# The transform back in runs of 128 columns and two 64-row tiles, the biases added to x on GpSimd, and the bias products between the runs

## The chip, the cores and the metric

The kernel runs on one core of one Trainium2 chip. The time is the device time of one execution in microseconds: 444.74 us in the median of 3 runs (444.65 to 445.85). The instructions and the queues of the five engines are written out by hand: PE is TensorE, ACT is ScalarE, DVE is VectorE, POOL is GpSimd, and SP only issues DMAs.

## The reference, cut to what matters

```
xf  = rfftn(gn(x).reshape(B, H, W, 4, 96), axes=(H, W), norm='ortho')      # 8 images, 32 x 32, 384 channels
r1  = relu(xr @ w1[0] - xi @ w1[1] + b1[0]);  i1 = relu(xr @ w1[1] + xi @ w1[0] + b1[1])
r2  = r1 @ w2[0] - i1 @ w2[1] + b2[0]
i2  = r2 @ w2[1] + i1 @ w2[0] + b2[1]                                       # r2 enters again
out = x + irfftn(r2 + 1j * i2) + gn(x) @ bias_w.T + bias_b                  # gn: 32 groups over H, W and 12 channels
```

Every float32 product is done as three float16 products of a high and a low part: high by high, high by low, low by high.

## The kernel before, in words

One image is one pass of `image(b, p)`, which each engine has for itself; semaphores alone tie the engines together, and each engine takes its instructions in the order written. On PE an image runs through these stages. `c1` multiplies y, the width transform of the normalised x, with w1. `p3_half` and `p3_last` transform along the height. `p1` already transforms the next image along the width. `p4` (L649) is the transform back: it takes r, the spectrum after the relu, as stationary and the table `heightT` as moving operand, so that the channels come to lie on the partitions, and makes rho. `c2_bias` (L688) multiplies y with the bias map, 18 products in pairs of 64-column tiles. `c2_rho` (L708) multiplies rho with w2 for each of 8 tiles gi. `mean` and `variance` of the next image stand between them, and `p6` ends the image.

p4 has ten runs j. The first eight take 96 columns of r each, which is one block of channels in its real or imaginary part, with 4 units by 3 products of 128 columns; the last two take unit 8, six products of 132 columns each. After each run ACT makes the high part of rho out of PSUM (L881, L887) and then DVE the low part (L1078, L1084). In the middle and at the end of the eight a copy of 12 columns moves on each of them (L884, L1081). A run waits for the evacuation of the run four before it (L667). One bias tile stands ahead of run 4 (L654), two behind run 9 (L751), and then PE waits for the whole of rho (L753).

DVE does `r_low(7)` and `r_low(8)` right ahead of its part of p4 (L1068, L1069). The bias vectors ride along in c2_rho: rows 96 to 98 of rho hold marks, loaded once (L502), and rows 96 to 98 of w2s hold b2 and bias_b (K = 99 in place of 96, L717).

Ahead of the first image DVE and POOL build w2f, the four forms of w2, with products on PE (L774 to L779, L805 to L807, L1161 to L1170). POOL finds the largest value over all partitions twice, with PARTITION_ALL_REDUCE (L800 and L814); the second one needs `largest_weight` and `largest_bias` of DVE (L1172, L1177), and DVE's `second_scales`, ACT's `weight_high` of the bias map and the rest of the first image need it. The output is made by `add_x` (L1032) out of the p6 product and x_sb, the x of this image. SP loads x of image b + 2 once image b is stored. Behind the last w1, w2, bias, table, b1 and x loads of the start SP issues eight small mark loads.

## Time and profile before

| what | value |
|---|---|
| median of 3 runs | 444.74 us |
| profiled execution, span from first to last instruction | 443.0 us |
| PE busy | 411.8 us (93%), 7832 products |
| PE weight loads busy | 375.5 us (85%) |
| DVE, ACT, POOL busy | 318.4 us (72%), 239.8 us (54%), 7.2 us (2%) |
| DMA | 32.50 MB, 20.1% of the 16 engines' time |
| bias products (1152), rho with w2 (3072) | 108.8, 84.5 us busy |
| transform back, p4 (864) | 52.3 us busy |

The median lies 1.7 us above the span: starting and ending a program is in it. A row of a group gives its line, its engine, what it writes and reads, the shapes, the count, the busy time, the mean of one and the idle time ahead of it with what ended that. A row of the timeline gives start and length in us. Products overlap, so the mean length of one (206 ns, say) is not its price; the price is the distance from start to start.

### The profile page before, as it was taken

Reading aid. Unit: us, or ns where it says so; the run is one execution under the profiler, and the core shown is the slowest. Engines: PE = TensorE matmul, PEld = TensorE weight load, DVE = VectorE, ACT = ScalarE, POOL = GpSimd, SP = SyncE. Lnnn points to the kernel's source line nnn. Section 1 sums busy time; section 2 is a strip of 40 time slices with the busy share of each in tenths; the row PEclk is TensorE's granted clock in tenths of the full one; section 3 lists DMA queues with packets and bytes.
Section 4 is the critical chain, followed back from the end, with each engine's and each line's share of the span. In section 5 each row is a group of like instructions: output and inputs, shape, how many; then the busy total and the mean of one; then the engine's idle time right before and its main releaser. Section 6 shows DMA issues by size and latency. Waiting matters only on the chain.

```text
span 443.0 us, 17840 instructions
## 1 busy us (share of the span) xinstructions
PE 411.8 (93%) x7832; PEld 375.5 (85%) x7832; DVE 318.4 (72%) x772; ACT 239.8 (54%) x568; POOL 7.2 (2%) x13
## 2 busy tenths in 40 slices
PE   4468699989999999999999999999999999998996
PEld 4457699889998899888998899888998899987894
DVE  3679895759776876769767786768857687668734
ACT  2654785257742685438752586438752577425620
POOL 0131000000000000000000000000000000000000
PEclk9759899999999999999999999999999999999999
DMA  7570000170004300170003500161002600030004
GB/s 216 164 216 2 2 1 4 63 261 3 3 23 157 148 1 5 38 285 3 3 12 123 194 1 4 38 243 45 2 5 88 236 1 4 27 155 3 4 4 144
DMA packets 11645, 32.50 MB, mean 73 GB/s; under 512 B 4196, under 2 KB 5904, under 8 KB 11568
## 3 DMA queue, kind: packets, MB, share of 16 engines
q1 hardware_dynamic: 11568, 31.36, 20.1%
q8 instruction: 62, 1.02, 1.0%
q14 instruction: 15, 0.12, 0.1%
HBM read 15.63 MB, written 12.58 MB: 64 GB/s over the span
## 4 chain that ended last, share of the span: by engine, by line
PE 81%; issue 7%; DVE 6%; SPq 2%; POOL 2%; ACT 1%; DVEq 0%; POOLq 0%
PE bank L535 81%; SPq L490 1%; DVE r L1022 1%; DVE z L947 1%; DVE rsum L1015 1%; SPq L495 1%; POOL g L806 1%; ACT biasw L857 1%; DVE o_sb L1037 0%; DVE rho L947 0%; POOL g L807 0%; ACT z L863 0%; ACT yraw L823 0%; DVE extreme L1175 0%; DVE extreme L1180 0%
## 5 line engine op out<-in xcount | busy, mean ns | idle before, releaser
L535 PE MATMUL bank<-biasw,y 128*64 128x384 f16 x1152 | 108.8, 335 | 0.0
L535 PEld LDWEIGHTS bank<-biasw,y 128*64 128x64 f16 x1152 | 93.5, 196 | 1.7 <-DVE rsum L1015 0.3
L535 PEld LDWEIGHTS bank<-w2s,rho 96*64 96x64 f16 (+1 forms) x3072 | 81.4, 109 | 4.4 <-issue 2.5
L535 PE MATMUL bank<-w2s,rho 96*64 96x96 f16 (+1 forms) x3072 | 84.5, 207 | 0.0
L863 ACT ACTIVATE z<-bank 128x384 f16<-128x384 f32 x72 | 35.2, 488 | 60.5 <-PE bank L535 59.9
L535 PE MATMUL bank<-w1R,y 128*32 128x96 f16 (+3 forms) x768 | 60.1, 228 | 7.6 <-ACT y L843 3.2
L848 ACT ACTIVATE g<-bank 128x384 f16<-128x384 f32 x64 | 31.0, 484 | 64.2 <-PE bank L535 64.2
L535 PE MATMUL bank<-tab,x_sb 128*128 128x128 f32 x384 | 52.5, 291 | 11.2 <-DMA x_sb<-in_x 6.6
L535 PEld LDWEIGHTS bank<-tab,x_sb 128*128 128x128 f32 x384 | 48.3, 201 | 14.6 <-issue 7.4
L947 DVE SCALAR_TENSOR_TENSOR rho<-bank,rho 96x64 f16<-96x64 f32 (+1 forms) x128 | 50.6, 431 | 10.9 <-PE bank L535 9.2
L947 DVE SCALAR_TENSOR_TENSOR z<-bank,z 128x384 f16<-128x384 f32 x72 | 39.9, 557 | 25.6 <-ACT z L863 25.2
L1029 DVE SCALAR_TENSOR_TENSOR g<-g,bank 128x384 f16<-128x384 f16 x64 | 34.8, 552 | 28.0 <-ACT g L848 27.6
L535 PE MATMUL bank<-w1I,y 128*128 128x192 f16 (+1 forms) x384 | 53.6, 249 | 0.0
L535 PEld LDWEIGHTS bank<-tab,r 128*96 128x96 f16 (+1 forms) x864 | 50.8, 124 | 2.5 <-issue 1.8
L535 PE MATMUL bank<-tab,r 128*96 128x128 f16 (+2 forms) x864 | 52.3, 221 | 0.4 <-DVE rsum L1015 0.4
L535 PEld LDWEIGHTS bank<-w1R,y 128*32 128x32 f16 (+3 forms) x768 | 38.2, 98 | 12.8 <-issue 7.8
L853 ACT ACTIVATE r<-rsum 128x384 f16<-128x384 f32 (+1 forms) x72 | 37.2, 519 | 9.9 <-DVE rsum L1015 9.1
L881 ACT ACTIVATE rho<-bank 96x480 f16<-96x480 f32 x64 | 35.1, 564 | 13.5 <-PE bank L535 9.5
L1037 DVE SCALAR_TENSOR_TENSOR o_sb<-bank,unscale,x_sb 128x384 f32<-128x384 f32 x64 | 35.0, 610 | 7.9 <-PE bank L535 7.9
L1022 DVE SCALAR_TENSOR_TENSOR r<-rsum,r 128x384 f16<-128x384 f32 (+1 forms) x72 | 37.4, 549 | 3.4 <-ACT r L853 2.7
L1015 DVE SCALAR_TENSOR_TENSOR rsum<-bank,b1s 128x384 f32<-128x384 f32 (+1 forms) x72 | 38.2, 547 | 0.0
L947 DVE SCALAR_TENSOR_TENSOR y<-yraw,rstd,y 128x1024 f16<-128x1024 f32 x24 | 30.9, 1292 | 8.0 <-ACT y L843 7.8
(102 smaller groups left out, 379.0 us busy)
## 6 DMA issues: line engine op xcount, KB each, us to landing
x_sb<-in_x SPq DMA_DIRECT2D x16, 768.0 KB, 7.1
out<-o_sb SPq DMA_DIRECT2D x14, 768.0 KB, 3.8
y<-y SPq DMA_DIRECT2D x24, 128.0 KB, 2.7
out<-o_sb SPq DMA_DIRECT2D x8, 192.0 KB, 1.9
tab<-in_tab SPq DMA_DIRECT2D x1, 642.0 KB, 5.9
o_sb<-in_bias_wt SPq DMA_DIRECT2D x4, 144.0 KB, 2.8
b1s<-in_b1h SPq DMA_DIRECT2D x1, 384.0 KB, 5.3
o_sb<-in_w SPq DMA_DIRECT2D x2, 144.0 KB
```

Source lines behind the costliest of these rows:

```text
L490: sp.dma_start(dst, src).then_inc(w1_in, 16)
L495: sp.dma_start(dst, src).then_inc(w2_in, 16)
L535: return nc.tensor.matmul(o, lhsT, rhs, start=start, stop=stop, **kw)
L848: nc.scalar.activation(g[:, 0, gi, :], g_bank(gi, more)[:, 0:CH], ACT.Copy, scale=G_EVAC).then_inc(gh_ready, 1)
L853: nc.scalar.activation(r[0:rows, 0, u, :], rsum[0:rows, u, :], ACT.Relu).then_inc(rh_ready, 1)
L863: nc.scalar.activation(z[:, 0, u, :], b_bank[u % 3][:, 0:CH], ACT.Copy, scale=Z_EVAC).then_inc(zh_ready, 1)
L881: nc.scalar.activation(rho_columns(0, j), rho_sums(bank), ACT.Copy, scale=H_EVAC).then_inc(rhoh_ready, 1)
L947: return nc.vector.scalar_tensor_tensor(out=out, in0=value, scalar=factor, in1=high, op0=ALU.mult, op1=ALU.subtract)
L1015: nc.vector.scalar_tensor_tensor(out=rsum[0:rows, u, :], in0=spec_bank(u)[0:rows, 0:CH], scalar=H_EVAC, in1=b1s[0:rows, u // 4, :], op0=AL ...
L1022: nc.vector.scalar_tensor_tensor(out=r[0:rows, 1, u, :], in0=rsum[0:rows, u, :], scalar=0.0, in1=r[0:rows, 0, u, :], op0=ALU.max, op1=ALU. ...
L1029: nc.vector.scalar_tensor_tensor(out=g[:, 1, gi, :], in0=g[:, 0, gi, :], scalar=-1 / G_EVAC, in1=g_bank(gi, more)[:, 0:CH], op0=ALU.mult, ...
L1037: nc.vector.scalar_tensor_tensor(out=o_sb[:, t, :].rearrange("k (p q) -> k p q", q=4), in0=o_bank[t % 4][:, 0:CH].rearrange("k (q p) -> k ...
```

## The change

In p4 the eight runs of 96 columns of r become six of 128 (j = 0 to 5, tile j % 3 of half j // 3). Each product is split into rows 0 to 63 and rows 64 to 127, with half of the table's columns each (64), into two banks that lie side by side; so a run has 24 products of 64 columns in place of 12 of 128. Unit 8 takes two runs (j = 6 and 7) with 24 products of 96 columns each, whose output tiles are 64 or 32 partitions wide. rho has three tiles of 128 partitions for each half in place of four blocks of 96. ACT reads one run with one instruction of 512 elements, DVE with two (256 and 224). The bias tiles stand ahead of runs 2, 4 and 6, and none behind the last run. c2_rho keeps its 48 products for each gi, now with 128 rows, some of them zero.

The marks and their rows go. What b2 and bias_b add to the output is a row for image row 0 and one for the others; PE and DVE work it out at the start (`shift_loads`, five float32 products, `shift_rows`, `shift_all`), and POOL adds it to x_sb in place for each image, once p1 has read it: one instruction of 384 and one of 2688 elements. add_x waits for that. The forms of w2 are all built by DVE, in 12 instructions (`second_forms`), and POOL's three instructions for them go. Loads at the start: w2 comes in twelve as before, but with 0.88 MB in place of 0.59; the float32 constants grow by 0.13 MB, and three loads (bias_all is 0.2 MB, b2col is 384 single words) replace the eight small ones of the marks.

```diff
+LOAD_PIECES = ((0, 0, 96, 0, 0, 0), (0, 96, 128, 0, 1, 0), (1, 0, 64, 0, 1, 32), (1, 64, 128, 1, 0, 0), (2, 0, 32, 1, 0, 64), (2, 32, 128, 1, 1, 0))
+WIDE_PIECES = ((0, 0, 64, 0, 0, 0), (1, 0, 64, 0, 1, 32), (1, 64, 128, 1, 0, 0), (2, 64, 128, 1, 1, 32))
+SMALL_PIECES = ((0, 64, 96, 0, 0, 64), (0, 96, 128, 0, 1, 0), (2, 0, 32, 1, 0, 64), (2, 32, 64, 1, 1, 0))
...
         def rho_bank(j, more):
+            if j < 6:
+                at = (2, 0 if more else 4)[j % 2]
+                return psum[:, at:at + 2, :]
+            return (b_bank[2] if more else c_bank[1], b_bank[0])[j - 6]
...
+            yield w2imag[:, :, :], w2[1].rearrange("b k n -> k b n")
+        def shift_loads():
+            yield b2rows[:, :], b2.rearrange("a b n -> a (b n)")
+            yield b2col[:, :], b2[0].rearrange("b n -> n b")
+            yield bias_all[:, :], bias_b.rearrange("(o n) -> o n", o=1).to_broadcast([128, CH])
...
+                        pe.wait_ge(w2_forms, 12)
+                        pe.wait_ge(added_ready, 6)
...
+                for j in range(8):
+                    if j in (2, 4, 6):
+                        gi = j // 2 - 1
+                        if more:
+                            c2_bias(b, p, gi, more, first)
+                        elif gi:
+                            c2_bias(b, p, 3 - gi, more, first)
+                    if j == 0:
+                        pe.wait_ge(spec_sum, 9 * b + 6)
+                    elif j == 1 and more:
+                        pe.wait_ge(y_raw, Y_ITEMS * (b + 1) + 5)
+                    elif j == 1:
                         pe.wait_ge(zh_ready, 9 * b + 9)
                         pe.wait_ge(zl_ready, 9 * b + 9)
+                        pe.wait_ge(spec_sum, 9 * b + 7)
+                    elif j < 6:
+                        pe.wait_ge(rhoh_ready, 8 * b + j - 1)
+                        pe.wait_ge(rhol_ready, 8 * b + j - 1)
+                    elif j == 6 and more:
+                        pe.wait_ge(y_raw, Y_ITEMS * (b + 2))
+                    elif j == 6:
+                        pe.wait_ge(spec_sum, 9 * b + 8)
+                    else:
+                        pe.wait_ge(rhoh_ready, 8 * b + 5)
+                        pe.wait_ge(rhol_ready, 8 * b + 5)
+                    if j in (0, 3, 6):
+                        pe.wait_ge(rh_ready, 9 * b + (4, 8, 9)[j // 3])
+                        pe.wait_ge(rl_ready, 9 * b + (4, 8, 9)[j // 3])
                     bank = rho_bank(j, more)
+                    if j < 6:
+                        ti = j % 3
                         for t in range(4):
+                            u = 4 * (j // 3) + t
+                            for of, w in ((0, 0), (0, 1), (1, 0)):
+                                for h in range(2):
+                                    rows = slice(64 * h, 64 * h + 64)
+                                    table = heightT[rows, w, int(u in SHORT_UNITS), :].rearrange("k (t c) -> k t c", t=TILES)[:, :, 8 * h:8 * h + 8]
+                                    o = bank[:, h, 0:256].rearrange("k (c u m) -> k c u m", u=4, m=4)[:, :, t, :]
+                                    last = mm(o, r[rows, of, u, 128 * ti:128 * ti + 128], table, of == 0 and w == 0, of == 1, skip_group_check=True)
                     else:
+                        half = j - 6
+                        for pieces in (WIDE_PIECES, SMALL_PIECES):
+                            for of, w in ((0, 0), (0, 1), (1, 0)):
+                                for tile, first_row, last_row, k, ri, ch in pieces:
+                                    at = BC * (2 * half + k) + ch
+                                    last = mm(bank[first_row:last_row, 0:384].rearrange("k (a t c) -> k a t c", a=3, c=32)[:, :, tile, :],
+                                              r[:, of, 8, at:at + last_row - first_row], xi[:, w, 96 * ri:96 * ri + 96], of == 0 and w == 0 and tile in (0, 1) and first_row == 64 * tile, of == 1, skip_group_check=True)
                     last.then_inc(rho_prod, 1)
...
+                                mm(columns[64:128], rhoX[:, of, half, tile, :], w2s[:, w, half, 0, slot, :], False, False, skip_group_check=True)
                             for part in range(2):
                                 at = 16 * (1 - part)
+                                last = mm(columns[64 * part:64 * part + 64], rho[:, of, half, tile, gi, at:at + 64],
+                                          w2s[:, w, half, part, slot, :], False, half == 1 and slot == 3 and of == 1, skip_group_check=True)
                 last.then_inc(g_prod, 1)
...
-                for gi in range(1, 3 if more else 2):
-                    c2_bias(b, p, gi, more, first)
-                pe.wait_ge(rhoh_ready, 10 * b + 10)
-                pe.wait_ge(rhol_ready, 10 * b + 10)
+                pe.wait_ge(rhoh_ready, 8 * b + 8)
+                pe.wait_ge(rhol_ready, 8 * b + 8)
...
+            for pieces in (WIDE_PIECES, SMALL_PIECES):
+                for tile, first_row, last_row, k, ri, ch in pieces:
+                    for half in range(2):
+                        blk = 2 * half + k
+                        last = mm(w2_product(tile)[first_row:last_row, half, :], w2T[:, blk, ri, ch:ch + last_row - first_row],
+                                  w2imag[:, blk, :], True, True, skip_group_check=True)
+            last.then_inc(w2_prod, 1)
+            pe.wait_ge(shift_in, 16 * N_SHIFT)
+            pe.wait_ge(added_ready, 1)
+            mm(c_bank[2][:, 0:CH], T("impulse", 2), b2rows[:, :], True, False, skip_group_check=True)
+            for blk in range(BLOCKS):
+                last = mm(c_bank[2][:, BC * blk:BC * blk + BC], b2row0[:, blk, :], w2imag[:, blk, :], False, blk == BLOCKS - 1, skip_group_check=True)
...
-            pool.wait_ge(w2_in, 16 * N_W2)
-            pool.wait_ge(consts_in, 16)
-            do(nc.gpsimd.tensor_copy(w2_form(0, BC, 0), by_group(w2raw[0:BC, :, 0, :])))
-            do(nc.gpsimd.tensor_scalar(w2_form(0, BC, 1), by_group(w2raw[0:BC, :, 1, :]), -1.0, None, ALU.mult))
-            do(nc.gpsimd.tensor_scalar(w2_form(BC, 3, 0), by_group(w2raw[BC:BC + 3, :, 0, :]), rowscale[BC:BC + 3, :], None, ALU.mult))
             pool.wait_ge(second_largest, 2)
-            do(nc.gpsimd.tensor_copy(extreme[BC:BC + 3, 4:5], extreme[BC:BC + 3, 2:3]))
-            do(nc.gpsimd.memset(extreme[BC:BC + 3, 2:3], 0.0))
             pool.wait_ge(s1_ready, 1)
-            do(nc.gpsimd.tensor_tensor(extreme[:, 2:5], extreme[:, 2:5], coef[:, 2:5], ALU.mult))
-            do(nc.gpsimd.tensor_scalar(extreme[:, 3:5], extreme[:, 3:5], s1[:, :], None, ALU.mult))
-            all_peak(extreme[:, 2:5], peaks2[:, :])
+            do(nc.gpsimd.tensor_tensor(extreme[:, 2:4], extreme[:, 2:4], coef[:, 2:4], ALU.mult))
+            do(nc.gpsimd.tensor_scalar(extreme[:, 3:4], extreme[:, 3:4], s1[:, :], None, ALU.mult))
+            all_peak(extreme[:, 2:4], peaks2[:, :])
+            pool.wait_ge(added_ready, 6)
+            for b in range(BATCHES):
+                pool.wait_ge(y_prod, Y_ITEMS * (b + 1))
+                tiles = x_sb[b % 2]
+                nc.gpsimd.tensor_tensor(tiles[:, 0, :], tiles[:, 0, :], added[:, 0, :], ALU.add).then_inc(x_shifted, 1)
+                nc.gpsimd.tensor_tensor(tiles[:, 1:TILES, :], tiles[:, 1:TILES, :], added[:, 1:2, :].to_broadcast([128, TILES - 1, CH]), ALU.add).then_inc(x_shifted, 1)
...
                     dve.wait_ge(stored[t // 4], 16 * b + 16)
...
+                    if j < 6:
+                        low(rho_columns(1, j)[:, 0], rho_sums(bank)[:, 0], H_EVAC, rho_columns(0, j)[:, 0])
+                        low(rho_columns(1, j)[:, 1, :, 0:28], rho_sums(bank)[:, 1, :, 0:28], H_EVAC, rho_columns(0, j)[:, 1, :, 0:28]).then_inc(rhol_ready, 1)
+                        if j % 3 == 2:
...
-                dve.wait_ge(pool_prep, 3)
+                dve.wait_ge(w2_prod, 1)
+                for part in range(2):
+                    for slot, tile, first_row, last_row in ((0, 0, 0, 128), (1, 1, 0, 64), (2, 1, 64, 128), (3, 2, 0, 128)):
+                        rows = slice(first_row, last_row)
+                        to, signs = w2_form(first_row, last_row, part, slot), sign[rows, tile:tile + 1]
+                        if part == 0:
+                            nc.vector.tensor_scalar(to, by_group(w2raw[rows, :, tile, :]), signs, None, ALU.mult).then_inc(w2_forms, 1)
+                            continue
+                        for half in range(2):
+                            nc.vector.scalar_tensor_tensor(out=to[:, half], in0=by_group(w2_product(tile)[rows])[:, half], scalar=signs,
+                                                           in1=by_group(w2real[rows, :, tile, :])[:, half], op0=ALU.mult, op1=ALU.add).then_inc(w2_forms, 1)
+            def shift_rows():
+                dve.wait_ge(shift_in, 16 * N_SHIFT)
+                row0 = T("row0", BC).rearrange("k (o m) -> k o m", o=1).to_broadcast([BC, BLOCKS, 128])
+                nc.vector.tensor_tensor(b2row0[:, :, :], row0, b2col[:, :].rearrange("k (b o) -> k b o", o=1).to_broadcast([BC, BLOCKS, 128]),
+                                        ALU.mult).then_inc(added_ready, 1)
+            def shift_all():
+                dve.wait_ge(shift_prod, 1)
+                for a in range(2):
+                    for of in range(2):
+                        parts = []
+                        for v in (added[:, a, :], bias_all[:, :], c_bank[2][:, 0:CH]):
+                            if len(parts) == 0:
+                                v = v.rearrange("k (c i q) -> k c i q", c=3, q=4)
+                                parts.append(v[:, :, :, 0:3] if of == 0 else v[:, :, :, 3])
+                            elif of == 0:
+                                parts.append(v[:, 0:3 * BC].rearrange("k (c i q) -> k c i q", c=3, q=3))
+                            else:
+                                parts.append(v[:, 3 * BC:CH].rearrange("k (i c) -> k c i", c=3))
+                        if a == 0:
+                            made = nc.vector.tensor_tensor(parts[0], parts[1], parts[2], ALU.add)
+                        else:
+                            made = nc.vector.tensor_copy(parts[0], parts[1])
+                        made.then_inc(added_ready, 1)
+                nc.vector.memset(newton[:, 0:1], 0.0).then_inc(added_ready, 1)
             def largest_weight():
+                dve.wait_ge(w2_forms, 12)
...
             image(0, 0, first=True)
             for b in range(1, BATCHES - 1):
```

## Rows read from the trace of the kernel before

**Rows 1.** The page: the span and the chain that ended last
```profile
span 443.0 us, 17840 instructions
...
PE 81%; issue 7%; DVE 6%; SPq 2%; POOL 2%; ACT 1%; DVEq 0%; POOLq 0%
```

**Rows 2.** Timeline of one image's transform back (start us, us, engine line, what)
```profile
207.23 2.85 PE L535 MATMUL bank<-tab,r 128*96 128x128 f16 x48
208.34 2.35 ACT L881 ACTIVATE rho<-bank 96x480 f16<-96x480 f32 x4
209.01 2.43 DVE L947 SCALAR_TENSOR_TENSOR rho<-bank,rho 96x480 f16<-96x480 f32 x4
210.01 1.74 PE L535 MATMUL bank<-biasw,y 128*64 128x384 f16 x18
211.48 0.26 DVE L1081 COPY rho<-rho 96x384 f16<-96x384 f16 x1
...
215.21 3.20 PE L535 MATMUL bank<-biasw,y 128*64 128x384 f16 x36
...
218.24 0.21 PE L535 MATMUL bank<-w2s,rho 99*64 99x96 f16 x1
```

**Rows 3.** Weight loads in groups, shapes kept apart (busy us, mean ns, then idle before)
```profile
L535 PEld LDWEIGHTS bank<-tab,r 128*96 128x96 f16 x672 | 43.5, 124 | 2.5 <-issue 1.8 <-DVE rsum L1015 0.7
...
L535 PEld LDWEIGHTS bank<-w1I,y 128*128 128x128 f16 x288 | 25.9, 100 | 0.2
```

**Rows 4.** Timeline of PE: rho with w2, products in two column tiles
```profile
221.97 1.23 PE L535 MATMUL bank<-w2s,rho 99*64 99x96 f16 x48
```

**Rows 5.** DVE in groups, shapes kept apart: the low part of rho
```profile
L947 DVE SCALAR_TENSOR_TENSOR rho<-bank,rho 96x480 f16<-96x480 f32 x64 | 39.9, 650 | 9.7 <-PE bank L535 9.2
...
L947 DVE SCALAR_TENSOR_TENSOR rho<-bank,rho 96x64 f16<-96x64 f32 x64 | 10.7, 212 | 1.2 <-ACT rhoX L887 1.2
```

**Rows 6.** Timeline of POOL at the start
```profile
16.90 0.86 POOL L805 COPY g<-o_sb 96x384 f32<-96x384 f32 x1 [4.26 <-issue]
26.21 2.55 POOL L806 TENSOR_SCALAR g<-o_sb 96x384 f32<-96x384 f32 x1 [8.45 <-issue]
28.86 1.58 POOL L807 TENSOR_SCALAR g<-o_sb,tab 3x384 f32<-3x384 f32 x1
...
38.88 0.68 POOL L812 TENSOR_TENSOR extreme<-extreme,tab 128x3 f32<-128x3 f32 x1
39.66 0.31 POOL L813 TENSOR_SCALAR extreme<-extreme,s 128x2 f32<-128x2 f32 x1
```

**Rows 7.** Chain that ended last: between POOL's L813 and its second all-reduce (peaks, L797)
```profile
40.21 6.00 issue
```

**Rows 8.** Timeline of DVE beside POOL at the start
```profile
27.27 1.52 DVE L947 SCALAR_TENSOR_TENSOR y<-yraw,rstd,y 128x1024 f16<-128x1024 f32 x1
...
38.70 0.81 DVE L1148 TENSOR_SCALAR b1s<-b1s,s 128x1152 f32<-128x1152 f32 x1
```

**Rows 9.** Group of those y instructions at the start, min/median/max ns
```profile
L947 DVE SCALAR_TENSOR_TENSOR y<-yraw,rstd,y x3: 1277/1285/1523, 24.9 to 27.3; 128x1024 f16<-128x1024 f32 x3
```

**Rows 10.** Timeline at the start: products for w2, the forms, the first z
```profile
21.34 2.91 PE L535 MATMUL bank<-o_sb,g 96*99 96x96 f32 x16
...
32.83 0.58 DVE L1170 TENSOR_SCALAR g<-o_sb,tab 3x384 f32<-3x384 f32 x1
33.45 1.02 DVE L947 SCALAR_TENSOR_TENSOR z<-bank,z 128x384 f16<-128x384 f32 x2
```

**Rows 11.** Windows: length, busy us (x) by engine, granted clock, DMA share, GB/s
```profile
25.00:30.00 5.00, 2.55 (x17) 2.38 (x18) 3.79 (x3) 2.27 (x3) 3.69 (x2) 0.50 0.90 306
30.00:35.00 5.00, 3.21 (x33) 2.92 (x31) 4.32 (x7) 1.03 (x3) 0.44 (x1) 0.89 0.12 36
```

**Rows 12.** Timeline of the next image's variance: its input on DVE, its use on PE
```profile
223.38 0.16 DVE L984 TENSOR_REDUCE qv<-qv 128x1 f32<-128x3 f32 x1
...
225.69 0.61 PE L535 MATMUL bank<-qv,tab 128*128 128x3 f32 x4
```

More of the change, by code:

```diff
@@ L188, in constants @@
     put("const", np.broadcast_to(const, (128, 64)))
-    tab[96:99, TAB["rowscale"][0]] = [ROOT, ROOT, 8.0]
-    put("coef", np.broadcast_to([1, 2.0 ** -8, 1, 2.0 ** -7, 2.0 ** -11], (128, 5)))
-    mark = np.zeros((3, TILES, 2, 2, 16))
-    mark[0, 0, 0, 0, :] = 1
-    mark[0, 0, 0, 1, 15] = 1
-    mark_a = mark.copy()
-    mark_a[1, 0, 0, 0, 15] = 1
-    mark_a[2, :, :, 0, 15] = 1
-    mark_a[2, 0, 0, 0, 15] = 0
-    mark_b = mark.copy()
-    mark_b[0, 0, 0, :, 15] = 0
-    extra = np.zeros((3, 64))
-    extra[1, 12] = 1
-    units_a, units_b = (m.reshape(3, TILES, 4, 4, 4).transpose(0, 1, 3, 4, 2).reshape(3, TILES, 4, 16) for m in (mark_a, mark_b))
-    marks = np.concatenate([np.concatenate([units_b[:, :, 3:4], units_a], axis=2).reshape(3, 640), extra], axis=1)
+    sign = np.ones((128, 3))
+    for tile, first, last, _, ri, _ in LOAD_PIECES:
+        if ri:
+            sign[first:last, tile] = -1
+    put("sign", sign)
+    put("coef", np.broadcast_to([1, 2.0 ** -8, 1, 2.0 ** -7], (128, 4)))
+    whole = np.ones((SIDE, SIDE // 2 + 1))
+    real, imag = (np.fft.irfftn(c * whole, s=(SIDE, SIDE), norm="ortho")[0] for c in (1, 1j))
+    impulse = np.zeros((2, 128))
+    impulse[0, 0:SIDE] = real
+    impulse[1, 0:SIDE] = imag
+    put("impulse", impulse)
+    put("row0", np.broadcast_to(impulse[1], (BC, 128)))
+    marks = np.zeros((1, 2))
     tab = tab.astype(np.float32)
@@ L234, in spectral_block_kernel @@
         r = sb("r", [128, 2, 9, CH], f16)
[L235 to L236 removed]
+        rho = sb("rho", [128, 2, 2, 3, TILES, 80], f16)
+        rhoX = sb("rhoX", [128, 2, 2, 3, 64], f16)
         g = sb("g", [128, 2, TILES, CH], f16)
@@ L409, in bias_loads @@
             yield biasraw[3:128:4, :, :], bias_wt[288:384, :].rearrange("(i b) n -> i b n", b=3)
[L411 to L416 removed]
+        N_W1, N_B1, N_W2, N_BIAS, N_SHIFT = (len(list(loads())) for loads in (w1_loads, b1_loads, w2_loads, bias_loads, shift_loads))
         N_ZERO = 6
@@ L501, in _ @@
             load(1, 1)
-            for dst, src in mark_loads():
-                sp.dma_start(dst, src).then_inc(marks_in, 16)
+            with nc.allow_non_contiguous_dma(reason="one column of 96 per block"):
+                for dst, src in shift_loads():
+                    sp.dma_start(dst, src).then_inc(shift_in, 16)
             def store(b, tiles=TILES // 2):
@@ L649, in p4 @@
             def p4(b, p, more, first):
-                for j in range(10):
-                    if j == 4:
-                        c2_bias(b, p, 0 if more else 2, more, first)
-                    if j == 3 and more:
-                        pe.wait_ge(y_raw, Y_ITEMS * (b + 2))
-                    elif j in (3, 4) and not more:
-                        pe.wait_ge(spec_sum, 9 * b + 4 + j)
-                    elif j < 2:
-                        pe.wait_ge(spec_sum, 9 * b + 5 + j)
-                    elif j == 2 and more:
-                        pe.wait_ge(spec_sum, 9 * b + 4)
-                    elif j == 2:
+                for j in range(8):
[10 more added lines that the diff above has]
+                    elif j == 1:
@@ L1201, in _ @@
             second_forms()
+            shift_rows()
+            shift_all()
             image(0, 0, first=True)
```

173 lines of the change are left out of this document (66 added, 107 removed).

## The prediction

> **What bounds the kernel now.** I read the page first: PE holds 81% of the chain that ended last, and what is left, DVE, POOL and time in which nothing is seen to be waited for, lies at the start [rows 1]. So a change counts where it shortens PE's queue or holds it up. Then the timeline of one image's transform back [rows 2]: its first product starts at 207.23 and the first of c2_rho at 218.24, 11.0 us later, and PE has no idle time in between. The double bias tile at 215.21 (3.20 us) covers the evacuation of the last runs. Then the start, where PE does not set the pace: DVE first reaches z at 33.45 [rows 10], and the second all-reduce on POOL waits 6.00 us in which nothing runs [rows 7].
>
> **Part 1, the products of p4.** Now 48 products take 2.85 us with the length of one, 0.22, at the end [rows 2], so 56 ns each: 128 columns at 2.4 GHz are 53. In c2_rho 48 products of 96 columns, two column tiles at a time, take 1.23 us with 0.21 at the end [rows 4]: 22 ns each, 43 a pair, where 96 columns are 40. So a pair costs its columns and some 3 ns, and the weight loads of both tiles lie beside that. A pair of the new products streams 64 columns in two row tiles: 29 ns, and a run of 12 pairs 0.35 us. The trace of before has no tiles of 64 rows by 128 columns; the other bound is that the 128 weights load at one column a cycle, 53 ns: 56 a pair, 0.67 a run. I take 29, since a load of 128 float16 columns lasts 100 ns and one of 96 columns 124 [rows 3]: a full width already loads in a faster way. Unit 8 has 24 small products a run: 12 at 22 ns, 12 four at a time at 11, and two changes of tile shape at some 0.15 each (a lone bias tile lasts 1.74, half of the double one 1.60 [rows 2]), so 0.68. The bias tiles now all stand alone: 3 x 1.75. PE's own work is 6 x 0.35 + 2 x 0.68 + 5.25 = 8.7 us in place of 11.0.
>
> **Part 2, what gives it back in each image.** No bias tile is left behind the last run, so its evacuation is in the open: 0.2 us until the product is in PSUM, three ACT instructions (0.45; four of 480 elements take 2.35 [rows 2]), three DVE instructions of 96, 96 and 6 elements (0.4; DVE takes 212 ns for 64 elements and 650 for 480, so 1.05 ns an element [rows 5]) and the semaphores, 1.15 us together. DVE can't start on rho before r_low(8) is done, at 209.01 [rows 2]; at 0.70 us a run (256 and 224 elements) it lets run 2 start at 209.8 and run 3 at 210.5, 0.45 us later than PE alone would. POOL slows DVE a little beside this (below), 0.2 to 0.3. Sum 10.6: **0.4 us less an image**, with bounds of 1.1 less (no waits on DVE, a short tail) and 1.0 more (56 ns a pair). c2_rho keeps its 48 products of 96 columns; 128 rows in place of 96 or 99 change nothing. The variance of the next image isn't late next: its input is there at 223.38 and PE takes it at 225.69 [rows 12].
>
> **Part 3, POOL's additions.** They are released when p1 is through; its last product ends at about 207.4, just as p4's first is under way [rows 2], and add_x needs them only at the image's end, so POOL's own time is hidden. What they do to DVE isn't. Price: a copy of 384 elements takes 0.86 us [rows 6], so 2688 take 6.0; by the row of 1.58 us for 384 it would be 11.1. I take 6.0, since these operands lie in order as that copy's nearly do. The two instructions then run until 214.4. (The Trainium skill, GPSIMD Engine Reference, section 3.1, gives 4497 ns for a tensor_tensor of 2048 float32 elements; by that it would be an estimated 5.9 us, and the sum stays.) On DVE L1148 does 1152 float32 elements in 0.81 us, faster than 1.05 ns an element [rows 8], and POOL's L812, three elements, starts under it at 38.88 and lasts 0.68, until DVE is done, while L813 right behind takes 0.31 [rows 6]. So a fast DVE instruction out of SBUF into SBUF and a POOL instruction exclude each other. In p4 DVE has one such: the copy L1081, 384 float16 elements in 0.26 [rows 2], now behind run 2's low part, at some 211.8. It would wait until 214.4; then come 0.2 for it and 0.7 for run 3's low part, until 215.3. Run 5 waits for that and would have started at 213.05. So **2.25 us are added, net 1.85 in each of the seven images** that hold additions for the next one. By POOL's two prices this is 0.4 to 7 us; in the last image 0.4 us are saved.
>
> **Part 4, the start.** (a) The forms of w2: DVE no longer waits for POOL's (28.86 + 1.58 [rows 6]) and starts at 28.8, as soon as the last y is done. Twelve instructions, by 0.58 for 384 elements [rows 10] some 0.36 for each of the four and 0.27 for each of the eight short ones, last until 32.3. Then shift_rows waits for its three loads, queued behind all others. The loads of before end at some 30.6 us (306 GB/s until 30, 36 GB/s after that [rows 11]); 0.3 to 0.6 MB more put that at 32 to 33.3. shift_rows (512 elements, 0.6), five float32 products on PE at half clock [rows 11] (16 of 96 columns took 2.91 [rows 10]; these are eight times 96 columns, 1.5), and shift_all (768 elements out of PSUM and SBUF, 1.5) end at 37.4. Queued behind these stand DVE's z and PE's c1, which now comes behind the five products. z started at 33.45: **4.0 us later**; bounds 2.5 (loads landed, short products) and 6. (b) POOL took 8.45 us ahead of L806 without a recorded reason, and 6.00 us ahead of the second all-reduce [rows 6, 7], each time where the kind of instruction changes between all-reduce and tensor operations; the copy L805 had none beyond its loads. I read that as code being fetched. Before, the first one lay under loads. Now the first tensor operation of POOL is the multiplication behind `second_largest`, so the fetch comes there, in front of everything that waits for the scales, and the second fetch stays. **6.0 us**, less 0.4 for the two small instructions dropped: 5.6. If the fetch is done ahead of that wait it costs nothing; I hold that for one in four.
>
> **The sum.** The profiled execution has 443.0, and 1.7 around it: 444.7, as the median. 444.7 + 4.0 + 5.6 + 7 x 1.85 - 0.4 = 466.9. The case's own range is 460 to 473.
>
> **Rivals.**
> R1, POOL disturbs nothing: no exclusion in this direction. For it: POOL's L806 ran beside a DVE instruction that then took 1523 in place of 1277 ns, 0.25 more and no wait of its length [rows 6, 8, 9]. Against it: L812. Each image then gains 0.2: 444.7 + 9.6 - 1.4 - 0.4 = 452.5; with the fetch hidden 446.9.
> R2, POOL holds back every DVE instruction with two operands in SBUF: r_low(8), due at some 208.5 as rho follows it at 209.01 [rows 2], would wait until 214.4 and all of rho's low parts with it. That is 5.9 us on the path, 5.5 net: 444.7 + 9.6 + 38.5 - 0.4 = 492. Against it speaks the 0.25 us [rows 9], for it the 2.55 us of L806 where 1.58 was enough for L807 [rows 6]. The Trainium skill (SBUF — State Buffer, section "SBUF: two separate sides") has this as its rule: an exclusive hold for the whole instruction, also against a DVE instruction with two SBUF inputs. The 0.25 us do not bear that out in full.
> R3, the row tiles load weights at one column a cycle, and POOL disturbs nothing: 1.0 more an image, 444.7 + 9.6 + 8.0 = 462.
> R4, the other side: nothing is held, POOL's fetch lies ahead of its wait, and the open tail and DVE's late start are covered, so an image keeps 1.1 us. With the cheap start it is 444.7 + 2.5 - 8.8 = 438. It turns at a start of more than 8 times the gain of an image.
>
> **How the numbers follow.** The forecast 0.38; the same with the fetch hidden (461) 0.10; R1 0.24 (a quarter of it at 447); R2 0.13; R3 0.05; R4 0.10. The range 447 to 490 leaves out R4, half of R2 and a little of R1: about 0.19. A measurement of this kernel can tell some 0.3%, 1.3 us, from no change: faster 0.11, same 0.05, slower 0.84.
>
> **What would show it.** Part 1: runs of 24 products in 0.35 us (plus 0.2 for the last to end), or 0.67. Part 2: some 1.2 us of PE idle ahead of each c2_rho, ended by DVE's rhoX. Part 3: POOL's long instruction at 6 us, DVE's copy behind run 2 starting late or lasting until POOL ends, and PE idle ahead of run 5; r_low as long as before speaks against R2. Part 4: DVE's first z at 37.4 and the second all-reduce's result at 55.8 in place of 46.2, with some 6 us of nothing ahead of POOL's multiplication. The prediction is wrong above all if DVE's copy goes through beside POOL, or if the fetch lies ahead of the wait.

## The result, and the profile after

The changed kernel takes 483.52 us in the median of 4 runs (482.19 to 487.52) beside 444.69 for the kernel before (441.99 to 445.85): a ratio of 1.0895, interval 1.0833 to 1.0957. It is slower by 39 us. The forecast was 467.0, with a range of 447 to 490. The profiled execution has a span of 484.8 us, 41.8 more than before [rows 1]. It was the longest of the four (487.52 us, 4.0 above their median), so the parts below add up to 41.8 us and not to 39.

The page of the changed kernel: span, engines (busy us, share of the span, instructions), the clock in 40 slices, the chain, and the two groups that the rest turns on.

```profile
span 484.8 us, 19207 instructions
PE 410.4 (85%) x8530; PEld 359.6 (74%) x8530; DVE 339.1 (70%) x768; ACT 228.6 (47%) x504; POOL 64.1 (13%) x24
...
PEclk9759968999899998999899998999899998999799
...
PE 67%; DVE 14%; ACT 9%; issue 8%; DMA 1%; DVEq 0%; SPq 0%; ACTq 0%
...
L552 PE MATMUL bank<-tab,r 64*128 64x64 f16 (+2 forms) x1536 | 38.2, 207 | 31.7 <-DVE rho L982 30.5
...
L849 POOL TENSOR_TENSOR x_sb<-x_sb,added 128x2688 f32<-128x2688 f32 x8 | 54.1, 6763 | 0.0
```

p4's products are busy for 38.2 us in place of 52.3, so the part that the change aims at got shorter. But PE now idles 30.5 us ahead of them for DVE's rho, its share of the chain fell from 81% [rows 1] to 67%, and the clock has a dent in each image. The same line of the page of before has one at the start only:

```profile
PEclk9759899999999999999999999999999999999999
```

Where the 41.8 us lie, by the first product of c1 in each image (before 87.8, 139.5, ... 393.16; after 102.64, 158.45, ... 430.87):

| stretch | before | after | more |
|---|---|---|---|
| start to p4 of the first image | 53.47 | 57.71 | 4.24 |
| p4 of the first image, to c2_rho | 11.76 | 22.50 | 10.74 |
| rest of the first image | 22.57 | 22.43 | -0.14 |
| images 1 to 6 | 305.36 | 328.23 | 22.87 |
| last image to the end | 49.84 | 53.93 | 4.09 |

One of the images 1 to 6 in the timeline (start us, us, engine line, what), to be read against [rows 2]:

```profile
175.14 2.40 DVE L1057 SCALAR_TENSOR_TENSOR r<-rsum,r 128x384 f16<-128x384 f32 x3
...
175.50 0.87 PE L552 MATMUL bank<-tab,r 64*128 64x64 f16 x48
...
175.65 1.00 POOL L848 TENSOR_TENSOR x_sb<-x_sb,added 128x384 f32<-128x384 f32 x1 [46.65 <-PE bank L552]
...
176.61 6.68 POOL L849 TENSOR_TENSOR x_sb<-x_sb,added 128x2688 f32<-128x2688 f32 x1
177.46 1.34 DVE L982 SCALAR_TENSOR_TENSOR rho<-bank,rho 128x256 f16<-128x256 f32 x4
178.32 1.11 PE L552 MATMUL bank<-tab,r 64*128 64x64 f16 x48 [0.27 <-DVE rho L982]
...
180.34 3.04 DVE L1118 COPY rho<-rho 128x288 f16<-128x288 f16 x1
...
184.16 0.53 PE L552 MATMUL bank<-tab,r 64*128 64x64 f16 x24 [2.60 <-DVE rho L982]
184.62 3.04 PE L552 MATMUL bank<-biasw,y 128*64 128x384 f16 x18
...
187.45 1.63 PE L552 MATMUL bank<-tab,r 128*64 128x96 f16 x48
...
190.34 0.20 PE L552 MATMUL bank<-w2s,rhoX 128*64 128x96 f16 x1 [1.25 <-DVE rhoX L982]
```

It reads like this. POOL's long addition ends at 183.29. DVE's copy of 288 elements, 0.24 us when alone (the second one of this image, at 186.18), begins at 180.34 and ends at 183.38. The low parts of rho, which read PSUM, run beside POOL at their usual length (four in 1.34 us, at 177.46). Run 5 needs what stands behind the copy, so PE idles 2.60 us. And then comes what the forecast did not have: the bias tile right behind takes 3.04 us in place of 1.74, because PE's clock has fallen. The window of that stretch (length, busy us and count of PE, PEld, DVE, ACT, POOL, granted clock, DMA share, GB/s):

```profile
185.00:190.00 5.00, 4.08 (x66) 2.81 (x62) 1.75 (x8) 2.09 (x9) 0.00 (x0) 0.67 0.01 3
```

The first image, where POOL adds the shift to images 0 and 1 one after the other:

```profile
58.54 1.00 POOL L848 TENSOR_TENSOR x_sb<-x_sb,added 128x384 f32<-128x384 f32 x1 [6.87 <-issue]
...
59.06 8.29 DVE L1057 SCALAR_TENSOR_TENSOR r<-rsum,r 128x384 f16<-128x384 f32 x3
...
59.51 6.15 POOL L849 TENSOR_TENSOR x_sb<-x_sb,added 128x2688 f32<-128x2688 f32 x1
...
66.89 7.92 POOL L849 TENSOR_TENSOR x_sb<-x_sb,added 128x2688 f32<-128x2688 f32 x1
...
69.00 1.34 DVE L982 SCALAR_TENSOR_TENSOR rho<-bank,rho 128x256 f16<-128x256 f32 x4
69.86 1.46 PE L552 MATMUL bank<-tab,r 64*128 64x64 f16 x48 [9.37 <-DVE rho L982]
```

Here r_low itself, with two operands in SBUF, is held: three of 0.55 take 8.29 us. The second long addition takes 7.92 us in place of 6.7; at its start DVE makes the low part of w2s (1.81 us, two operands in SBUF).

The start:

```profile
31.54 0.68 DVE L1216 TENSOR_TENSOR b2row<-tab,b2col 96x512 f32<-96x512 f32 x1
32.37 1.61 PE L552 MATMUL bank<-b2rows,tab 2*128 2x384 f32 x2 [8.34 <-DVE b2row L1216]
33.91 2.02 PE L552 MATMUL bank<-g,b2row 96*128 96x96 f32 x8
35.97 0.69 DVE L1234 TENSOR_TENSOR added<-bias_all,bank 128x288 f32<-128x288 f32 x2 [3.75 <-PE bank L552]
...
38.49 0.56 DVE L982 SCALAR_TENSOR_TENSOR z<-bank,z 128x384 f16<-128x384 f32 x1 [1.42 <-ACT z L898]
...
44.22 0.19 POOL L840 TENSOR_TENSOR extreme<-extreme,tab 128x2 f32<-128x2 f32 x1 [31.21 <-DVE extreme L1248]
...
51.30 0.37 POOL L832 PARTITION_ALL_REDUCE peaks<-extreme  x1 [5.86 <-PE bank L552]
```

The forms of w2 are done at 31.7. z comes at 38.49 in place of 33.45. POOL's multiplication follows DVE's last maximum (ending at 44.07) by 0.15 us, so no fetch lies there; the one ahead of the all-reduce is as long as before, 5.86 us.

### The profile page after: what moved, and what is told of

Its sections match the earlier page's. It is cut to its first block, busy times and chain, and to the rows that moved or that the text cites. A ratio compares the mean times of both kernels' runs of the same rounds, so it can differ in the third digit from the quotient of the medians.

```text
span 484.8 us, 19207 instructions
## 1 busy us (share of the span) xinstructions
PE 410.4 (85%) x8530; PEld 359.6 (74%) x8530; DVE 339.1 (70%) x768; ACT 228.6 (47%) x504; POOL 64.1 (13%) x24
## 4 chain that ended last, share of the span: by engine, by line
PE 67%; DVE 14%; ACT 9%; issue 8%; DMA 1%; DVEq 0%; SPq 0%; ACTq 0%
PE bank L552 67%; DVE r L1057 4%; DVE rho L982 3%; ACT r L888 3%; ACT yraw L858 2%; DVE rsum L1050 2%; DVE z L982 1%; ACT rho L916 1%; DMA x_sb<-in_x 1%; ACT z L898 1%; ACT rho L922 1%; DVE y L982 1%; ACT junk L866 1%; ACT biasw L892 0%; DVE g L1209 0%
## 5 line engine op out<-in xcount | busy, mean ns | idle before, releaser
L552 PE MATMUL bank<-biasw,y 128*64 128x384 f16 x1152 | 119.6, 357 | 0.2 <-DVE biasw L982 0.2
L552 PE MATMUL bank<-w2s,rho 128*64 128x96 f16 x3072 | 83.1, 208 | 0.4 <-issue 0.4
L552 PEld LDWEIGHTS bank<-w2s,rho 128*64 128x64 f16 x3072 | 79.1, 109 | 4.7 <-issue 3.0
L552 PE MATMUL bank<-tab,r 64*128 64x64 f16 (+2 forms) x1536 | 38.2, 207 | 31.7 <-DVE rho L982 30.5
L552 PEld LDWEIGHTS bank<-tab,r 64*128 64x128 f16 (+2 forms) x1536 | 31.9, 104 | 42.4 <-issue 32.2
L982 DVE SCALAR_TENSOR_TENSOR rho<-bank,rho 128x256 f16<-128x256 f32 (+2 forms) x128 | 40.0, 360 | 33.1 <-ACT rhoX L922 17.5
L552 PE MATMUL bank<-w1R,y 128*128 128x192 f16 (+3 forms) x768 | 59.7, 228 | 3.4 <-issue 2.9
L849 POOL TENSOR_TENSOR x_sb<-x_sb,added 128x2688 f32<-128x2688 f32 x8 | 54.1, 6763 | 0.0
L916 ACT ACTIVATE rho<-bank 128x512 f16<-128x512 f32 x48 | 27.4, 592 | 47.0 <-PE bank L552 47.0
L552 PEld LDWEIGHTS bank<-w1R,y 128*128 128x128 f16 (+3 forms) x768 | 38.0, 98 | 6.2 <-issue 4.7
```

Of the source, the lines that this page charges most:

```text
L552: return nc.tensor.matmul(o, lhsT, rhs, start=start, stop=stop, **kw)
L849: nc.gpsimd.tensor_tensor(tiles[:, 1:TILES, :], tiles[:, 1:TILES, :], added[:, 1:2, :].to_broadcast([128, TILES - 1, CH]), ALU.add).then_i ...
L916: nc.scalar.activation(rho_columns(0, j), rho_sums(bank), ACT.Copy, scale=H_EVAC).then_inc(rhoh_ready, 1)
L982: return nc.vector.scalar_tensor_tensor(out=out, in0=value, scalar=factor, in1=high, op0=ALU.mult, op1=ALU.subtract)
```

## The experiments

Each is compared with the kernel before, run on the same chip; ratios carry their 95% interval. p4 means the time from p4's first product to the first of c2_rho in one of the images 1 to 6: 11.01 before, 14.8 after.

**e1_no_add: without POOL's additions.** The loop of POOL and add_x's wait for it are gone; the kernel leaves out what b2 and bias_b add to the output.

```diff
-            for b in range(BATCHES):
-                pool.wait_ge(y_prod, Y_ITEMS * (b + 1))
...
-                dve.wait_ge(x_shifted, 2 * b + (1 if t == 0 else 2))
```

> The changed kernel without POOL's additions and without add_x's wait for them; the output lacks what b2 and bias_b add. Theory A (POOL's instructions shut out DVE, and only that makes the images longer): p4's first product to c2_rho's first falls from 14.8 us to about 10.6, an image from 54.3 to about 50.1 (50.5 in the kernel before), DVE's copy takes 0.24 us, and the kernel 447 to 450 us, the start's 5 us included. Theory B (the new p4 itself, its open tail and the clock that falls behind it, makes the images longer): an image stays above 53 us and the kernel above 470.

450.82 us, ratio 1.0094 (1.0065 to 1.0124). p4 takes 10.23, an image 49.7 us in place of 50.5, and the second image starts at 94.4 (before 87.8, after 102.6). So of 39 us the additions in their place are some 35, by the two ratios. What is left is made of three parts (spans 448.0 and 443.0): +6.6 up to the second image, -5.5 in images 1 to 6, +3.9 in the last. p4 of the first image takes 13.3 here, 11.8 before and 22.5 with the additions: of the 10.7 us more in the table, 9.2 are the additions and 1.5 the new order.

**e2_add_in_c1: the same additions, later.** POOL waits for the next image's c1 in place of p1. A second wait keeps the first image's additions (in eight pieces) behind its rho.

```diff
-                pool.wait_ge(y_prod, Y_ITEMS * (b + 1))
+                if b:
+                    pool.wait_ge(z_prod, 9 * b + 1)
+                else:
+                    pool.wait_ge(rhol_ready, 8)
```

> POOL's additions are released at the first c1 unit of the image whose x they change, not behind its p1; in c1 DVE has no instruction with two SBUF operands and no fast copy. Those of the first image come behind rho in eight pieces. Theory A: as without the additions, within 2 us of that run: 448 to 452 us, with POOL's long instruction at some 6 us and z's low parts as long as before (0.55). A rival C, that POOL slows all of SBUF's users whatever they run: z's low parts, ACT and PE lengthen under it and some 3 us an image stay, 470 us or more.

452.59 us, 1.0122 (1.0058 to 1.0186): 1.3 us more than without additions by the ratios, which is less than their intervals can tell, with the same p4 of 10.23. So the additions cost almost nothing here: it is their place that costs. In c1 DVE makes z and rsum, all of it out of PSUM, and POOL's instruction is shorter there:

```profile
197.62 5.88 POOL L856 TENSOR_TENSOR x_sb<-x_sb,added 128x2688 f32<-128x2688 f32 x1
```

**e3_pieces: the long addition in seven.** Eight instructions of 384 elements, where they stood.

```diff
+                for t in range(TILES):
+                    nc.gpsimd.tensor_tensor(tiles[:, t, :], tiles[:, t, :], added[:, min(t, 1), :], ALU.add).then_inc(x_shifted, 1)
```

> The additions stay behind p1, but in eight instructions of 384 elements of some 1.0 us each, 8 us in all in place of 7.7. If what shuts DVE out lasts as long as one POOL instruction, DVE's copy and r_low wait for one piece at most (1 us or less) and PE's clock does not fall: 0.5 to 1.5 us an image more than without additions, 452 to 462 us. If it is the total work of POOL that counts, 480 us or more.

459.23 us, 1.0266 (1.0210 to 1.0322); p4 11.21. The work on POOL is the same, the hold is not:

```profile
170.77 1.03 DVE L1118 COPY rho<-rho 128x288 f16<-128x288 f16 x1
...
172.58 0.53 PE L552 MATMUL bank<-tab,r 64*128 64x64 f16 x24 [0.59 <-DVE rho L982]
173.03 1.74 PE L552 MATMUL bank<-biasw,y 128*64 128x384 f16 x18
```

The pieces of this image by themselves (ns min/median/max):

```profile
L849 POOL TENSOR_TENSOR x_sb<-x_sb,added x8: 992/1001/1781, 166.1 to 173.6; 128x384 f32<-128x384 f32 x8
```

The copy waits for one piece and gets in between two. PE's wait is 0.59 and the bias tile keeps its 1.74: at this wait the clock stays. POOL goes on adding until 174.6 and DVE and PE go on beside it, so what costs most is the length of one POOL instruction and not how much POOL adds. The pieces still cost 7.6 us by the ratios of e3 and e1, 1.0 in each p4 of the images 1 to 6.

**e4_before_add: the kernel before, with additions of zero.** The two additions of the changed kernel on a tile of zeros, nothing else.

> The kernel before, with POOL adding zeros to x_sb by the same two instructions, released in the same place, and add_x's wait; nothing else changed. Theory A: DVE's copy behind the fourth run (0.26 us) lasts until POOL is done, some 3.5 us later; the double bias tile covers part of it, so 1 to 3 us an image, and several us in the first image, where r_low meets the long instruction: 455 to 470 us. Theory B: within 2 us of the kernel before.

462.1 us, 1.0311 (1.0233 to 1.0388). p4 is 12.2 in place of 11.0, and 23.0 in the first image in place of 11.8. The timeline of an image:

```profile
169.77 6.71 POOL L824 TENSOR_TENSOR x_sb<-x_sb,added 128x2688 f32<-128x2688 f32 x1
...
172.99 3.61 DVE L1092 COPY rho<-rho 96x384 f16<-96x384 f16 x1
...
177.32 0.52 PE L538 MATMUL bank<-tab,r 128*96 128x132 f16 x6 [1.05 <-DVE rho L957]
177.77 3.20 PE L538 MATMUL bank<-biasw,y 128*64 128x384 f16 x36
```

The same hold, 3.61 us, stands in front of PE as 1.05, since the old p4 has more work between the copy and what needs it; the double bias tile keeps its 3.20. So the additions cost the old order 14 us by the ratio (18.9 by the spans, 11.5 of them in the first image) and the new one 35. The difference lies in the images 1 to 6: there they cost the old p4 1.2 us and the new one 4.6. A faster p4 is also a p4 in which PE has less work of its own to put over another engine's delay.

**e5_filler: PE kept busy during its wait.** Sixteen products that nobody reads stand ahead of run 5's wait (in the bank that run 6 writes next, once y has been read out of it).

```diff
+                        if j == 5 and more:
+                            pe.wait_ge(y_raw, Y_ITEMS * (b + 2))
+                            for i in range(16):
+                                mm(b_bank[2][:, 0:CH], inv[:, 0, 1, :], z[:, 0, i % 8, :], True, True)
```

> The changed kernel with 16 products of 384 columns, whose result nobody reads, issued by PE ahead of its wait for run 5, in the bank that run 6 will overwrite: 2.6 us of work in a wait of 2.6 us. The wait stays as it is. If a part of the loss is PE's clock, which falls after that wait, the bias tile behind run 5 goes from 3.04 back to 1.74 us, an image from 54.3 to 52.3 to 52.8, and the kernel from 484 to 468 to 474. If the clock's fall costs nothing or has another cause, the time stays within 3 us of 484.

478.52 us, 1.0754 (1.0695 to 1.0813): above what was expected of the whole, since the first and the last image keep their losses, but the image is as expected, 52.8 in place of 54.3.

```profile
179.88 3.05 DVE L1122 COPY rho<-rho 128x288 f16<-128x288 f16 x1
...
181.03 2.77 PE L552 MATMUL bank<-z,tab 128*128 128x384 f16 x16
...
184.19 1.74 PE L552 MATMUL bank<-biasw,y 128*64 128x384 f16 x18
...
185.76 1.28 PE L552 MATMUL bank<-tab,r 128*64 128x96 f16 x48
```

The copy is held as before (3.05) and run 5 starts as late, but the bias tile takes 1.74 and unit 8's runs 1.28 in place of 3.04 and 1.63. PE did more work and the kernel got faster. So of the 4.6 us that p4 is longer with additions (14.8 against 10.23), 3.0 are the hold (13.26 against 10.23) and 1.5 the clock that falls behind it.

**e6_act_copy: the held copy on ACT.** DVE's two copies (L1118) are made by ACT, the additions stay.

```diff
-                            nc.vector.tensor_copy(rho_third(1, j // 3, 0), rho_third(1, j // 3, 64))
+                            act.wait_ge(rhol_ready, 8 * b + 3)
+                            nc.scalar.activation(rho_third(1, 0, 0), rho_third(1, 0, 64), ACT.Copy)
```

> The changed kernel, but the copy of 12 columns of rho's low part is done by ACT (behind its own part of runs 3 and 6), so that DVE has nothing of the fast kind in p4; POOL's additions stay behind p1. If in the later images the copy alone is shut out, an image falls from 54.3 to 50 to 51, while the first image, where r_low meets the long instruction, stays long: 457 to 462 us. If POOL holds all of DVE's work, an image stays above 53 us.

460.54 us, 1.0346 (1.0281 to 1.0411); p4 10.58.

```profile
176.75 0.44 ACT L922 ACTIVATE rho<-rho 128x288 f16<-128x288 f16 x1
177.45 0.90 PE L552 MATMUL bank<-tab,r 64*128 64x64 f16 x48
178.28 1.74 PE L552 MATMUL bank<-biasw,y 128*64 128x384 f16 x18
```

ACT makes the same copy in SBUF beside POOL in 0.44 us, and run 5 follows run 4 without a wait. This one copy was nearly the whole hold of the images 1 to 6 (10.58 against 10.23 without additions). The first image keeps its 21.4, where r_low is what is held.

**e7_c1_start: e2, with the start rearranged.** The five shift products go behind the third unit of the first c1, `shift_all` behind DVE's fifth z, and p3 waits for it.

> As e2_add_in_c1, and the five float32 products for the added rows stand behind the third c1 unit on PE (which waits for DVE there anyway), shift_all behind scale_b1 on DVE. The start's 5 us consist of PE's wait for those products (3.7 us from shift_rows to shift_all on DVE) and shift_all; this should return 3 to 4.5 us: 447.5 to 449.5 where e2 has 452.6. If the start is set by the second all-reduce's code alone, nothing.

451.33 us, 1.0142 (1.0093 to 1.0192) against e2's 1.0122: the expected return of 3 us and more did not come. c1 starts at 26.49 in place of 36.22, and the shift products take 1.9 us in place of 3.6 (31.86 to 33.80), but then PE stands still until `shift_all` has read their bank:

```profile
39.79 1.07 PE L552 MATMUL bank<-z,tab 32*32 32x384 f16 x45 [3.01 <-issue]
```

The products behind that wait run slowly (45 in 1.07 us, 0.79 in e10). The second image starts 3.2 us earlier in this profile, and that image and the last one give it back (2.3 and 0.9). In the second image PE idles 1.75 us in the middle of c1, where e2 has 0.88 and the profile names no releaser in either:

```profile
103.46 0.20 PE L552 MATMUL bank<-w1R,y 96*32 96x96 f16 x1 [1.75 <-issue]
```

Behind it the clock is lower (0.67 in the window from 105 to 110), which in e2 it is not; 0.9 us of wait and the slow products make up the 2.3.

**e8_c1_start_tail: e7, with the bias tiles placed for cover.** The third bias tile goes behind run 7, where it covers the last evacuation; in the last image the two tiles that are left stand ahead of runs 2 and 4.

```diff
-                    if j in (2, 4, 6):
+                    if j in (2, 4):
...
                 p4(b, p, more, first)
+                if more:
+                    c2_bias(b, p, 2, more, first)
```

> As e7_c1_start, with the third bias tile behind the last run of p4 in place of ahead of run 6, and in the last image bias tiles ahead of runs 2 and 4. The open tail (1.3 us of PE idle ahead of c2_rho) is covered, at the price of 0.2 us of wait ahead of run 7: 0.7 to 1.0 us an image less, and 3 us in the last image, where PE's clock fell: 438 to 442 us, faster than the kernel before. If the tail is set by DVE and not by what PE has to do, an image stays at 49.7 and the kernel at 444 to 446.

444.52 us, 0.9988 (0.9952 to 1.0024): 39 us faster than the changed kernel and level with the one before, but not the 438 to 442 that were expected. p4 is 9.61 in place of 10.23, as expected, and the images behind it take 49.1 to 49.7. What is missing to that lies before: the second image takes 52.3, with 2.04 us of idle time at the same place of c1 as in e7 and a lower clock behind it, and the first one has the start that e10 below mends.

**e11_tail: e2 with that tail alone.**

> This is e2 (additions during c1) with the tail of e8 alone: the third bias tile goes behind p4's run 7, so that it covers the last evacuation, and in the last image the two bias tiles that are left stand ahead of runs 2 and 4. The start is as in the changed kernel. Theory A: the open tail cost 0.6 us in each of seven images (10.23 against 9.61 of p4 in e7 and e8) and the missing cover in the last image some 3.2: 452.6 - 4.3 - 3.2 = 445. Rival B, that e8's last image owed its gain to something else in its start: 448 to 449.

445.54 us, 1.0030 (0.9996 to 1.0063): against e2 4 us less by the ratios, 7 by the medians, so e8 owed its gain to the tail. Between e11 and e8, which has e7's start on top, lie 2 us by the ratios, and their intervals overlap. In the last image of e2 and then of e11:

```profile
414.39 1.46 PE L552 MATMUL bank<-tab,r 64*128 64x64 f16 x48 [3.37 <-DVE rho L989]
415.78 2.69 PE L552 MATMUL bank<-biasw,y 128*64 128x384 f16 x18
```

```profile
406.09 1.74 PE L552 MATMUL bank<-biasw,y 128*64 128x384 f16 x18
409.53 1.11 PE L552 MATMUL bank<-tab,r 64*128 64x64 f16 x48 [1.70 <-DVE rho L991]
410.57 1.74 PE L552 MATMUL bank<-biasw,y 128*64 128x384 f16 x18
```

Without a bias tile between runs 1 and 2, PE waits 3.37 us for DVE, and the tile behind runs slowly. With it, p4 of the last image takes 11.24 in place of 13.38. (The spans hide that: in e11's profile 4.2 us pass from DVE's last instruction to the end, in the others of these kernels 2.4.)

**e10_start_bank: e8, with the shift products in a bank of their own.** They go into the bank of the next image's first p1, and the wait for `shift_all` moves from p3 to that p1.

```diff
-                        pe.wait_ge(added_ready, 6)
+                    if first and m == 0:
+                        pe.wait_ge(added_ready, 6)
```

> This is e8 with one more move at the start. In e8 PE idled 3.06 us ahead of p3 (41.02), since p3 waited for shift_all to have read the bank of the shift products (DVE L1245, L1247, until 40.75), while the z that p3 needs was there at 37.2. Here the five shift products go into the bank that nothing uses until the next image's p1 (46.06 in e8), and the wait stands ahead of that p1. Theory A, that the start was set by this wait and by the clock that fell behind it (c1's products at 690 ns in place of 410 from 42.2 to 45): the idle time ahead of p3 goes, the first image is 2.5 to 3.5 us shorter, 441 to 442.5 in all, faster than the kernel before. Rival B, that the first image is set by the second all-reduce on POOL (45.68 in e8, 5.9 us of fetch ahead of it) and what follows from it: what is saved ahead of p3 comes back as idle time ahead of p4's bias tile or its run 2, and the time stays at 444 to 445.

441.95 us, 0.9921 (0.9888 to 0.9954): faster than the kernel before (445.07 in these runs) by 3.1 us of the medians, and the fastest of all. p3 follows c1, whose last product starts at 36.93, at once:

```profile
37.11 0.79 PE L552 MATMUL bank<-z,tab 32*32 32x384 f16 x45
```

The second image starts at 88.3 (e8 93.9, before 87.8), so the start now costs 0.5 us more than in the kernel before. By the profiles (438.3 against 443.0) the six images give 8.9 and the last one still takes 3.6.

## Why the prediction was right or wrong

The side was right and the time lies in the range, 16.5 us above the forecast and 8.5 below R2's 492. Step by step:

**Part 1** held. A run of 24 row-tile products takes 0.52 us with its last product's 0.2, as forecast, and two runs 0.87: 29 ns a pair. R3 (56 ns) is out.

**Part 2** had the right items and too small a gain. Forecast 10.6, measured 10.23 in e1: 0.8 us an image in place of 0.4. The open tail is there (1.25 us ended by rhoX, forecast 1.15). DVE's late rho, forecast at 0.45, costs nothing without POOL: in e1 run 2 starts 2.57 us behind p4's first product, with no wait, and in the changed kernel 2.82 us behind it. Those 0.27 us of wait are POOL's doing, through r_low(7) below. e8 shows the tail from the other side: covered, it gives 0.62 back.

**Part 3**, the hold, is right in its mechanism in images 1 to 6: the copy behind run 2's low part waits until POOL ends, 3.04 us, and run 5 with it. Two terms were off. POOL ended later, at 7.8 us from p4's start in place of 7.2: alone it takes 5.88 us, close to the forecast 6.0, but in p4 6.68. The hold costs 3.0 in place of 2.25. And a term was missing: the clock, 1.5 us an image. Net 3.8 an image in place of 1.85: 11.8 us over six images.

**Part 3 in the first image** failed. It was counted like the others, at 1.85. There POOL does two images in one go, and the long instruction is under way when r_low comes. R2's hold then acts: 9.2 us of the 10.7 by e1. The other 1.5 are the new order by itself, which the forecast did not have in this image either: in e2 PE waits 2.91 us there for the low part of rho, which stands behind w2s on DVE. In the other images r_low all but escapes (0.7 us) by its order, not because it is allowed beside POOL:

```profile
L1057 DVE SCALAR_TENSOR_TENSOR r<-rsum,r x3: 544/545/1251, 175.1 to 177.0; 128x384 f16<-128x384 f32 x2, 96x384 f16<-96x384 f32 x1
```

The one of 96 partitions, r_low(7), takes 1251 ns: it begins under POOL's short addition and is over some 0.4 us after it. r_low(8) follows at 177.0 and takes its usual 545, though the long addition has begun at 176.61. I read this as DVE being let in between POOL's two instructions and the long one waiting for it, since that one takes 0.8 us more than in c1, and so does one of e3's eight pieces (1781 in place of 1001 ns). The first image of e4 shows the same hold of POOL by DVE more plainly: the short addition, 1.0 us alone, lasts 3.06 us while DVE ends r_low(8) and makes w2s.

```profile
61.87 3.06 POOL L823 TENSOR_TENSOR x_sb<-x_sb,added 128x384 f32<-128x384 f32 x1
62.28 1.80 DVE L957 SCALAR_TENSOR_TENSOR w2s<-g,w2scale,w2s 99x1536 f16<-99x1536 f32 x1
```

The Trainium skill (SBUF — State Buffer, section "SBUF: two separate sides") calls it an exclusive lock: whichever instruction starts first has the shared ports for its whole length. By the 8.29 us the trace agrees. I weighed the wrong row against R2: the 0.25 us of [rows 9] beside L806 don't fit the rule, and are not explained by what was run here, but L806's own 2.55 [rows 6] and L812 spoke for it.

**Part 4 (a)** had the right chain and one term too small: forms until 31.7, loads no wait at all, shift_rows 0.68, but the five float32 products last 3.6 us in place of 1.5 and z comes 5.0 later in place of 4.0. In e7, where PE comes to them from c1 and not from 8.34 us of idling, they take 1.9. **Part 4 (b)** was wrong, in the way named as one chance in four: the fetch lies ahead of the wait. POOL's first tensor operation follows its releaser by 0.15 us. Of the 5.6 us nothing came. Both together: p4 starts 4.2 us later in place of 9.6.

**The last image** was forecast at -0.4 and costs +4.1. The change put its tiles so that none stands between runs 1 and 2 there; I costed the seven other images' order and did not write out this one.

The sum as measured by the spans is 41.8. The forecast had 9.6 + 1.85 + 11.1 - 0.4 = 22.15, so its errors worked against each other: 5.4 too much at the start, and behind it too little by 8.8 in the first image (10.6 against 1.85), 11.8 in the six and 4.5 in the last. That part is luck: with the start forecast as it came, the number would have been 461.6, 22 us too low. R1 (452.5) stands for a POOL that disturbs nothing. e1 and e2 took 450.8 and 452.6, but that is near by luck as well, since R1 counts 5.6 us of fetch that did not come and gives the last image 0.4 us less where it takes 3.9 more. R4 was not this kernel; e10 shows what remains when nothing is held and the tail is covered.

Of the last image's 3.6 us in e10 some 2.3 are the clock: its windows from 405 to 415 show 0.66 and 0.73, and e8, which has the same order there and kept the clock, takes 1.3 us more than the kernel before. What stays open: why the wait of 1.70 us in e10 was followed by a lower clock and the one of 1.71 in e8 was not, and what PE waits for in c1 of the second image.

## What to carry to other kernels

Before work goes to an idle engine, list what DVE does beside POOL in that stretch, instruction by instruction; put the long instruction where DVE reads PSUM, or cut it into pieces (35 us of cost became 1.3, too little to be told from none, in one case and 8 in the other). Price a wait on the critical engine with its after-effect: behind the waits of 2.6 us the slow products cost another 1.5. And write out the order of the special images, the first and the last, as carefully as that of the others: here they held 15 of 42 us.

## What was not expected of the hardware

- A wait of PE of 2.60 us was followed by products at the lower of the two levels, 1.2 GHz in place of 2.4, in each of the images 1 to 6 (a bias tile in 3.04 us in place of 1.74, granted clock 0.67 in its window), and so was one of 3.37 in the last image of e2. Useless products in the wait (2.77 us) kept the clock, and made the kernel 5 us faster.
- The length of a wait did not decide this alone. Behind a wait of 2.7 us in the first image, eight float32 products took 2.08 us in e10 and 1.16 in e2; behind e2's wait of 2.91 us, also in the first image, the clock stayed (granted clock 1.00 from 60 to 70). Of three waits of 1.7 us, in the last images of e8, e10 and e11, only e10's was followed by the lower clock (bias tile 2.66). The waits of 0.59 and 1.05 shown above were not.
- POOL's addition of 2688 float32 elements in place, one operand broadcast, takes 5.88 us in c1, 2.19 ns an element, and 6.68 in p4; one of 384 takes 1.0.
- A copy inside SBUF on DVE is held by POOL for as long as it runs (3.04 us in place of 0.24), and so is one with two operands in SBUF (r_low, three in 8.29 us); the same copy on ACT (0.44 us) and DVE's instructions that read PSUM (1.34 for four) are not. DVE's instructions with two operands in SBUF held POOL in turn (3.06 us in place of 1.0).
- The time that POOL takes where its kind of instruction changes was hidden under a long wait (0.15 us from DVE's maximum to POOL's product), and open ahead of the all-reduce (5.86) and of the first addition (6.87, under other work).
